# A graph kernel's edge sort, spread over three hops: counting product one block later, half blocks begun 7, 11 and 8

## The reference

```python
for _ in range(3):
    msg = (x * norm_out[:, None])[src]
    agg = jax.ops.segment_sum(msg, dst, num_segments=N)
    x = 0.5 * (agg * norm_in[:, None]) + 0.5 * h0
...
x = _layernorm(x0 + x @ W.T)
h = jax.nn.relu(jnp.concatenate([x[src], x[tgt]], axis=1) @ W1 + b1)
w = jax.nn.sigmoid(h @ W2 + b2)[:, 0]
agg = jax.ops.segment_sum(w[:, None] * x[src], tgt, num_segments=x.shape[0])
```

## Time and profile before

| | |
|---|---|
| median of 3 runs | 1120.77 us (1120.27 to 1121.59) |
| profiled execution | 1122.8 us, span 1121.1 us |
| mean granted TensorE clock | 0.946 |
| busy in the span | PE 947.2 us, DVE 956.2, ACT 614.6, POOL 496.5 |
| hops 1 to 3 in the span | about 212 to 540 us |

### The profile page before, as it was taken

The page is one execution under the profiler, slowest core; times in us unless marked ns, Lnnn a source line. Parts: engine busy times, 40 slices in busy tenths (PEclk is TensorE's granted clock), DMA queues, the critical chain, the costliest instruction groups (busy, mean ns, idle before and its releaser), DMA issues.

```text
span 1121.1 us, 33394 instructions
## 1 busy us (share of the span) xinstructions
PE 947.2 (84%) x11292; PEld 785.8 (70%) x11293; DVE 956.2 (85%) x2664; ACT 614.6 (55%) x1523; POOL 496.5 (44%) x676
## 2 busy tenths in 40 slices
PE   4889898787889888989479999999989999989950
PEld 2888888576677767777257787877767777777740
DVE  7999999589999998987479999998878888888866
ACT  6666776512100002222267777887767767767755
POOL 1000000300101003546777777777777777777711
PEclk9999999799999999999689999999989999999975
DMA  3000000000000000111476777777767776767601
GB/s 103 1 1 0 0 0 0 1 1 3 3 2 3 3 3 18 40 45 47 121 217 204 205 219 211 221 212 216 206 191 209 212 206 200 206 207 207 184 12 49
DMA packets 77517, 117.44 MB, mean 105 GB/s; under 512 B 20489, under 2 KB 38973, under 8 KB 77373
## 3 DMA queue, kind: packets, MB, share of 16 engines
q1 hardware_dynamic: 58172, 63.13, 18.8%
q0 software_dynamic: 19200, 52.45, 16.6%
HBM read 108.66 MB, written 6.86 MB: 103 GB/s over the span
## 4 chain that ended last, share of the span: by engine, by line
DVE 37%; POOL 26%; issue 16%; PE 15%; ACT 3%; DMA 1%; SPq 1%; DVEq 1%; ACTq 0%; POOLq 0%
POOL region L889 17%; POOL U L889 6%; PE bank L1772 5%; DVE stage L995 4%; DVE hx L995 3%; DVE aggT L1192 3%; DVE stage L1158 3%; DVE aggT L1167 2%; POOL stage L889 2%; DVE aggT L995 2%; DVE stage L1179 1%; DVE t L1251 1%; ACT region L2000 1%; PE bank L1869 1%; DVE t L1249 1%
## 5 line engine op out<-in xcount | busy, mean ns | idle before, releaser
L889 POOL DMA_INDIRECT region<-src_split,region x272 | 266.2, 979 | 84.8 <-issue 81.9
L1772 PE MATMUL bank<-U,region 128*128 128x256 f16 (+1 forms) x1875 | 236.8, 277 | 3.4 <-DVE U L1135 2.1
L1772 PEld LDWEIGHTS bank<-U,region 128*128 128x128 fp8e4 x1875 | 180.6, 99 | 37.3 <-DVE U L1135 2.8
L2186 ACT CAST region<-bank 128x512 f16<-128x512 f32 x338 | 180.7, 591 | 0.0
L2036 ACT CAST region<-bank 128x500 f32 x202 | 120.0, 594 | 56.0 <-PE bank L1661 46.6
L2166 ACT ACTIVATE region<-bank 128x512 f16<-128x512 f32 x169 | 100.9, 597 | 64.6 <-PE bank L1872 59.7
L1449 DVE SCALAR_TENSOR_TENSOR region<-bank,region 128x512 f16<-128x512 f32 x169 | 116.4, 688 | 15.9 <-ACT region L2166 12.4
L1869 PE MATMUL bank<-region,xs 128*128 128x256 f16 x676 | 106.0, 281 | 18.5 <-DVE region L1449 11.5
L1433 DVE TENSOR_SCALAR region<-region,stage 128x512 f16<-128x512 f16 x338 | 108.8, 363 | 9.8 <-DMA region<-slot_rows 9.8
L889 POOL DMA_INDIRECT U<-src_split,region x96 | 93.0, 969 | 29.3 <-issue 29.3
L1881 PE MATMUL bank<-U,region 128*128 128x256 f16 x676 | 105.9, 281 | 0.0
(11 more groups left out here) (293 smaller groups left out, 2320.2 us busy)
## 6 DMA issues: line engine op xcount, KB each, us to landing
region<-slot_rows SPq DMA_DIRECT2D x169, 256.0 KB
region<-in_dst_dram SPq DMA_DIRECT2D x100, 64.0 KB
region<-src_split,region POOLq DMA_INDIRECT x272
slot_rows<-aggT SPq DMA_DIRECT2D x104, 3.2 KB
src_split<-U SPq DMA_DIRECT2D x25, 64.0 KB, 1.5
src_split<-xs SPq DMA_DIRECT2D x25, 64.0 KB, 1.5
tgt_split<-q SPq DMA_DIRECT2D x25, 64.0 KB, 1.6
region<-tgt_split SPq DMA_DIRECT2D x100, 16.0 KB
```

Of the source, the lines that this page charges most:

```text
L889: nc.gpsimd.indirect_dma_start(out=rows_of(n, i), out_offset=None, in_=src_split, in_offset=bass.IndirectOffsetOnAxis(ap=listed[n % LISTS] ...
L1772: z = nc.tensor.matmul(bank[2 * (k % 2) + p][:, 0:width], count[:, h, b * P:(b + 1) * P], U[k % 2][:, h, 0:width], start=h == 0, stop=h == ...
L2186: nc.scalar.copy(y_rows[u % 4][:, a, :], bank[3 + a][:, :]).then_inc(rows_copied, 1)
```

## The change

The steps at which half blocks begin come from three runs instead of one: 7 in hop 1 (steps 3, 6, 9, 12, 15, 18, 21), 11 in hop 2 (25, 27, 29, 31, 34, 36, 38, 40, 43, 45, 47), 8 in hop 3 (50, 52, 54, 56, 59, 61, 63, 65). Before they were 9, 10 and 7 (3, 5, 8, 10, ... 23; 25, 28, ... 48; 50, 53, 55, 58, 60, 63, 66). The counting product and all that follows it (numbers, places, fill, turn, copies, stores) come one step later; scan and loads keep their lags. Nothing is added or removed. Lines below 106 stand six lines further down in the new file.

```diff
+    SORTED_2, SORTED_3 = min(HALF_BLOCKS * 3 // 7, 12), 8
+    SORTED = ((HALF_BLOCKS - SORTED_2 - SORTED_3, 3, NB - 3), (SORTED_2, NB, NB), (SORTED_3, 2 * NB, NB - 7))
+
     def sorted_at(hs):
 
-        return 3 + hs * (2 * NB + 13) // (HALF_BLOCKS - 1)
+        for size, first, blocks in SORTED:
+            if hs < size:
+                return first + hs * blocks // size
+            hs -= size
...
             def sort_vector(s):
                 judge_input(s)
-                hs = sort_of(s, 4)
+                hs = sort_of(s, 5)
                 if hs is not None:
                     sort_places(hs)
-                hs = sort_of(s, 3)
+                hs = sort_of(s, 4)
                 if hs is not None:
                     sort_numbers(hs, s)
                 hs = sort_of(s, 2)
...
             def sort_products(s):
-                hs = sort_of(s, 2)
+                hs = sort_of(s, 3)
                 if hs is not None:
                     count_earlier(hs, s)
-                hs = sort_of(s, 6)
+                hs = sort_of(s, 7)
                 if hs is not None:
                     fill_slots(hs, s)
-                hs = sort_of(s, 7)
+                hs = sort_of(s, 8)
                 if hs is not None:
                     turn_slots(hs, s)
```

More of the change, by code:

```diff
@@ L105, in due @@
         return n if left == 0 and 0 <= n < end else None
+    SORTED_2, SORTED_3 = min(HALF_BLOCKS * 3 // 7, 12), 8
+    SORTED = ((HALF_BLOCKS - SORTED_2 - SORTED_3, 3, NB - 3), (SORTED_2, NB, NB), (SORTED_3, 2 * NB, NB - 7))
     def sorted_at(hs):
-        return 3 + hs * (2 * NB + 13) // (HALF_BLOCKS - 1)
+        for size, first, blocks in SORTED:
+            if hs < size:
+                return first + hs * blocks // size
+            hs -= size
     def sort_of(s, lag):
         return next((hs for hs in range(HALF_BLOCKS) if sorted_at(hs) + lag == s), None)
-    assert all(sorted_at(hs + 1) - sorted_at(hs) >= 2 for hs in range(HALF_BLOCKS))
+    assert all(sorted_at(hs + 1) - sorted_at(hs) >= 2 for hs in range(HALF_BLOCKS - 1))
     def tiles_in(n):
@@ L665, in _ @@
                 tables(c, c % 2)
-                hs = sort_of(2 * NB + c, 6)
+                hs = sort_of(2 * NB + c, 7)
                 if hs is not None:
@@ L1747, in sort_products @@
             def sort_products(s):
-                hs = sort_of(s, 2)
+                hs = sort_of(s, 3)
                 if hs is not None:
                     count_earlier(hs, s)
-                hs = sort_of(s, 6)
+                hs = sort_of(s, 7)
                 if hs is not None:
                     fill_slots(hs, s)
-                hs = sort_of(s, 7)
+                hs = sort_of(s, 8)
                 if hs is not None:
                     turn_slots(hs, s)
-            offs_before = sum(sort_of(s, 2) is not None for s in range(2 * NB))
-            fills_before = sum(sort_of(s, 6) is not None for s in range(2 * NB))
-            turns_before = sum(sort_of(s, 7) is not None for s in range(2 * NB))
+            offs_before = sum(sort_of(s, 3) is not None for s in range(2 * NB))
+            fills_before = sum(sort_of(s, 7) is not None for s in range(2 * NB))
+            turns_before = sum(sort_of(s, 8) is not None for s in range(2 * NB))
             def hop(k, b, p):
```

## The result

The changed kernel takes 1127.01 us (median of 4 runs, 1126.15 to 1127.67), the kernel before 1120.52 beside it (1119.19 to 1121.59): ratio 1.0058, 95% interval 1.0041 to 1.0076, so 6.5 us slower. The forecast was 1121.5.

What follows compares the result with a forecast made beforehand. DVE was taken to fill the hops, with only its idle time to win. Hops 1 to 3 summed -16.1 + 5.0 + 11.8 = +0.7 us on a median of 1120.77, giving 1121.5, range 1116.3 to 1126.5.

Steps and rivals of the forecast that it cites:

- DVE fills the hops: Hops 1 to 3: DVE's work stays the same and only moves; only its idle time, 18.5 us, could be won.
- a wait at the counting product in hop 2: Hop 2: PE still waits there, since numbers of the half block before come only one step ahead.
- loads do not wait for whole fills: Hops 2 and 3: nine loads wait about 0.2 us each for a fill, not 1.33 each (12 in all).
- the keys of half block 21: Hop 3, step 55: keys waiting for late loads hold GpSimd's splits, ScalarE's copy and DVE's Q sum; 2.7 us idle.
- the sum of DVE's idle time in hop 3: Hop 3: 12.9 us idle after the change, +5.1, within a hop sum of +11.8.
- two steps without sort work: Hop 3, steps 53 and 62: DVE idles ahead of the next drain, twice 2.2 us.
- keys of 24 and 25: Hop 3: these keys stand ahead of splits 9 and 11, waiting for loads at steps 61 and 63; 0.4 and 1.3 us.
- start of hop 3: Start of hop 3: DVE's idle time falls from 2.3 to 0.6 us as places fill it.
- small pieces: Hop 3: some 3.5 us of idle time stay at blocks with a fill, 7 of them at about 0.5.
- rival C: Hop 3: TensorE's clock falls after PE waits at steps 54, 56, 63, 65; +4.5, 1126 in all; chance 0.20.
- A: Hop 3: GpSimd hold-ups don't reach DVE, 4.4 us less, 1117.1 in all; chance 0.17.
- B: Hops 1 to 3: PE is the bound and all 27.9 us of waits at the counting product go, 1093; chance 0.03.

Runs made afterwards that it cites:

- run 6: Changed kernel with 18 unused matmuls at the head of step 63 (block 13 of hop 3): 1125.88 us, ratio 1.0026 to the kernel before.
- run 3: Changed kernel with four buffers for keys instead of two: 1122.12 us, ratio 1.0006 to the kernel before.
- run 4: Changed kernel with DVE's write of y (nodes 0 to 11) behind the first part of the sort work: 1128.89 us, ratio 1.0053.
- run 5: Changed kernel with four buffers for keys and, for all nodes, y written behind the first part of the sort work: 1122.05 us, ratio 0.9995.
- run 7: Changed kernel with four buffers for keys and 18 unused matmuls at the head of step 63: 1121.71 us, ratio 0.9994.
- run 1: Kernel before with its table kept, the counting product and all behind it one step later: 1121.67 us against 1121.53, ratio 1.0001.
- run 8: Kernel before with its table kept, the later lags for half blocks 0 to 17 only: 1116.82 us against 1122.66, ratio 0.9945.

## Why the prediction was wrong

**What held.** That DVE fills the hops and its work only moves (hop 1 -16.5 for -16.1, hop 2 +5.3 for +5.0, with 2.9 us idle for 3.0; in hop 1 two small misses cancel, 10.9 us less busy time for 11.5 and 5.5 less idle for 4.6); that PE keeps a wait at the counting product in hop 2; that loads do not wait for whole fills; the price of the keys of half block 21 (2.83 for 2.7) and of the first step without sort work (2.28 for 2.2).

**The step that failed** is the sum of DVE's idle time in hop 3, forecast at 12.9 us. The gaps in DVE's rows up to drain 71 make 18.2, and these 5.3 us are nearly the whole miss of 5.5:

| term | forecast | measured |
|---|---|---|
| two steps without sort work | 4.4 | 2.28 + 4.38 = 6.7 |
| keys of 21 | 2.7 | 2.8 |
| keys of 24 and 25 | 1.7 | 1.46 + 0.95 = 2.4 |
| start of hop 3 | 0.6 | 0.73 + 0.45 = 1.2 |
| small pieces | 3.5 | 5.1 |

The largest is the drain behind step 62. I took its price from the earlier trace rows, where PE's clock is whole, and gave the clock to rival C as something apart, at 1.56 us in each of the steps 54, 56, 63 and 65. C's mechanism came true once in the profiled execution, beyond the start of the hop, whose first 20 us run at 0.91 in both kernels. It came at none of those steps but behind step 61, and cost 2.7 us (run 6). At two of C's four steps PE did wait, 1.85 and 2.25 us, without a fall. Step 61 is not on C's list, which looks for numbers, loads and scan together; it has places, loads and scan, and takes 6.37 us. So the forecast left the clock out where it fell, and the rival had it at the wrong steps and, with fill and eleven matmuls alone, too cheap. The keys are mis-sized too: their stalls on DVE sum to 5.2, and freeing them took 6.6 off hop 3 (run 3), 0.6 of the rest by a shorter wait at drain 63 (3.78 us) and 0.7 by shorter busy time of DVE. Four small pieces of 0.35 or 0.36 are loads that wait for a fill in hop 3; I had left only about 0.5 at each of 7 blocks for all that.

**The rivals.** A (the keys don't reach DVE) is refuted by the three waits ahead of the Q sum and by run 3. B (PE is the bound) gave 1093: 11.7 of the 27.9 us at the product went, and the kernel became slower; in hop 2, where 10.4 us of such waits are left, DVE is busy 96.4 of 103.7 us and PE 88.6. C is right in kind, with 0.20, but that its 1126 is near the 1127 is in part luck: it gave the clock 4.5 us on top of a forecast that was too low by other terms as well, and the clock cost 2.7.

The Trainium skill's "TensorE: Matmul & The Clock Gate", section "HAM oscillation — how this bites in real kernels", describes slow matmuls behind idle gaps; the waits of the case in that section are some 3 to 5 us. The trace agrees in kind at 476.86 and, by run 6, that the gap is the cause, but here gaps of about 2 us were enough; and gaps of 2.25 us without a fall at 492.87 and with one in run 6 show that the length alone does not tell which gap it will be.

**What stays open**: which of several 2 us waits lets the clock fall. It fell at step 63 in all four profiles of the changed table that had a wait of 2.0 us or more there (the change itself, runs 3 to 5) and not in the two with work in it (runs 6 and 7). But it fell elsewhere in runs 1, 4, 6, 7 and 8, behind waits of 1.98 to 2.60 us, and the same wait at the same place let it fall in one execution and not in another (2.25 us in run 6 and the changed kernel, 2.02 in runs 7 and 3). So a single profile of hop 3 holds some luck. Nor do the runs tell the small pieces and the start of the hop apart, 2.2 of the 5.3 us.

## What to carry to other kernels

Where one engine is full, a new table moves its work and can only win or lose its idle time; so ask of each step of the new table what stands together in it, and who waits behind. A lag and a spacing go together: here the lags alone changed nothing, the table alone cost 2.7%, and lags chosen by hop won 0.55%. Look first for in-order queues held by one early wait (twice the buffers for keys gave back nearly 6 of 6.5 us), and price the steps in which PE stands still at both clocks.

## What was not expected of the hardware

TensorE's clock fell behind waits of only 2 us in otherwise busy work: 1.98 us in run 8, 2.02 in run 7, 2.25 in run 6, 2.26 in the changed kernel. It did not fall behind the same waits in other executions: 1.97 in the kernel before, 2.03 and 2.25 in the changed kernel. The slow stretch in the changed kernel lasted some 6 us (from the fill at 479.19 to drain 63 at 485.35) and cost 2.7 there, the one in run 6 cost 0.5. Eighteen matmuls of no use in the wait kept the clock up at step 63 and were free: PE takes up the row of y 0.02 us behind drain 62 with them and without.
